# A convolution, attention and routing block on one core: the next pair's correlations put ahead of the logits, reciprocal deviations taken by a power on GpSimd, two norm groups summed back to back, fewer waits at the first K tile

## The reference

```python
def conv(x):                                  # x is the group-normalised input
    t1 = stack([pad(x)[..., 2*k:2*k+w] for k in range(7)])     # seven shifted copies
    t2 = conv_1x3(x, w2)
    t3 = einsum('nakhw,nbhw->nakb', t1, x) / sqrt(h*w)         # the correlations
    t9 = p9w * p6w * t3
    t10 = einsum('nakb,nakhw->nbhw', t9, shifted(t2)) / sqrt(c*7)
    return depthwise_5x5_dilated(x, w8) - (t10 - depthwise_1x5(t2, w7))
x = x + conv(group_norm(x))                   # 32 groups of 2 channels
t = tokens(x)
t = t + attention(layer_norm(t))              # 16 heads of 64; features elu+1 times cos, sin of
                                              # the position; keys x values summed over all tokens
t = t + ffn(layer_norm(t))                    # 32 experts: logits over all tokens, a softmax over the
                                              # tokens, the best 8 tokens of each expert are weighted
# layer_norm: (v - mean) / sqrt(var + eps) over the 64 channels of a token
```

## Time and profile before

| | us |
|---|---|
| median of 3 runs | 4075.51 (4073.82 to 4081.14) |
| the profiled execution | 4079.0 |
| its span, first to last instruction | 4077.2 |
| TensorE busy | 3586.0 (88%) |
| VectorE busy | 2994.3 (73%) |
| ScalarE busy | 1687.9 (41%) |
| GpSimd busy | 1248.6 (31%) |
| mean granted TensorE clock | 0.94 of full speed |

### The profile page before, as it was taken

How to read it: one execution, slowest core, us unless ns; L and a number is a source line. 1 busy time by engine, 2 the same in 40 slices (tenths; PEclk the granted TensorE clock), 3 DMA queues, 4 the chain that set the end, 5 groups by cost and what they waited for, 6 DMA issues and landing times.

```text
span 4077.2 us, 52073 instructions
## 1 busy us (share of the span) xinstructions
PE 3586.0 (88%) x17556; PEld 1798.3 (44%) x17556; DVE 2994.3 (73%) x3523; ACT 1687.9 (41%) x1798; POOL 1248.6 (31%) x1327
## 2 busy tenths in 40 slices
PE   4798998989889998989889899899989898899976
PEld 2344444444544444444444445344444444544453
DVE  6878876788677876788767886778767887548823
ACT  0145533455254534445434553445435554343310
POOL 1015620176013740156201760127501572011100
PEclk8899998999999998999989999999989999899967
DMA  1000000000000001000000000000010000100045
GB/s 47 17 1 1 1 17 25 1 1 1 25 17 1 1 1 41 1 1 1 17 25 1 1 1 25 17 1 1 1 41 1 1 1 16 30 1 1 1 116 200
DMA packets 18676, 70.96 MB, mean 17 GB/s; under 512 B 8781, under 2 KB 13421, under 8 KB 13485
## 3 DMA queue, kind: packets, MB, share of 16 engines
q1 hardware_dynamic: 18365, 67.10, 5.3%
HBM read 37.26 MB, written 29.84 MB: 16 GB/s over the span
## 4 chain that ended last, share of the span: by engine, by line
issue 48%; PE 33%; DVE 8%; POOL 7%; ACT 2%; DMA 1%; SPq 1%; POOLq 0%; DVEq 0%; ACTq 0%
PE ps_D L1499 11%; POOL UA L549 4%; PE ps_E L1463 4%; PE ps_C L1488 3%; PE ps_A L1446 3%; PE ps_B L1446 3%; DVE RR L1106 2%; PE ps_E L1474 1%; DVE region L1076 1%; DVE arena L911 1%; PE ps_C L1417 1%; POOL RS L581 1%; PE ps_E L1512 1%; POOL RR L574 1%; DVE region L1085 1%
## 5 line engine op out<-in xcount | busy, mean ns | idle before, releaser
L562 POOL TENSOR_TENSOR arena<-arena,UHL 128x896 f32<-128x896 f32 x350 | 764.6, 2210 | 226.3 <-ACT UHL L695 211.6
L1499 PE MATMUL ps_D<-region,small 128*128 128x448 f32 x1792 | 785.2, 562 | 32.9 <-DVE OS L1112 32.8
L549 POOL TENSOR_TENSOR UA<-region,CS 128x128 f32<-128x128 f32 (+1 forms) x400 | 178.8, 449 | 1837.8 <-DVE region L986 795.3
L1085 DVE TENSOR_TENSOR region<-region,ps_C 128x896 f32<-128x896 f32 x448 | 485.9, 1085 | 247.9 <-PE ps_C L1488 247.9
L1499 PEld LDWEIGHTS ps_D<-region,small 128*128 128x128 f32 x1792 | 321.2, 194 | 346.7 <-issue 284.8
L734 ACT ACTIVATE EQ<-ps_B,NEG 128x896 f32<-128x896 f32 x224 | 225.6, 1007 | 480.4 <-PE ps_B L1446 480.3
L911 DVE SCALAR_TENSOR_TENSOR arena<-arena,W8C 128x896 f32<-128x896 f32 (+1 forms) x418 | 416.8, 1010 | 1.2
L1417 PE MATMUL ps_C<-region,UA 128*128 128x512 f32 (+1 forms) x800 | 382.7, 601 | 2.9 <-ACT region L627 2.9
L734 ACT ACTIVATE EQ<-ps_A,NEG 128x896 f32<-128x896 f32 x224 | 225.6, 1007 | 350.8 <-PE ps_A L1446 350.7
L695 ACT ACTIVATE UHL<-arena,W8C 128x896 f32<-128x896 f32 x350 | 361.2, 1032 | 0.0
L1052 DVE SCALAR_TENSOR_TENSOR region<-region,ps_B 128x1024 f32<-128x1024 f32 (+1 forms) x200 | 243.9, 1219 | 159.8 <-ACT region L713 156.4
(11 more groups left out here) (310 smaller groups left out, 5772.9 us busy)
## 6 DMA issues: line engine op xcount, KB each, us to landing
arena<-x SPq DMA_DIRECT2D x8, 1568.0 KB, 6.6
t_keep<-Y SPq DMA_DIRECT2D x7, 1568.0 KB, 6.8
w_keep<-region SPq DMA_DIRECT2D x7, 784.0 KB, 5.7
CST<-t_keep SPq DMA_DIRECT2D x2, 1568.0 KB, 10.0
small<-t_keep SPq DMA_DIRECT2D x2, 1568.0 KB, 12.8
...
```

Source lines behind the costliest of these rows:

```text
L562: pool.tensor_tensor(out=X[:, cut], in0=X[:, cut], in1=PRODUCT[m % 3], op=ALU.add).then_inc(pool_taps.sem, 1)
L1085: dve.tensor_tensor(out=q, in0=q, op=ALU.mult, in1=here.area(key)[:, :].rearrange("p (c n) -> p c n", c=2)[:, :, 0:PIX])\
L1499: ins = pe.matmul(here.area(key)[:, 0:PIX], MW[i][:, c, :], Q[s % 3][:, c, :], start=c == 0, stop=c == NCHUNK - 1)
```

## The change

Six things change:

- **Correlations ahead.** In the loop, TensorE runs `correlations` (37 transposes and 124 matmuls) after the last slot of the Q loop, ahead of the tokens' transposes and logits; before, they came after the logits. ScalarE's copies (now `columns`) move with them.
- **The boundary's order.** TensorE no longer has the routing weights and the pooled tokens ahead of the convolution, but after its third part. VectorE does the residual of part 0 between match-replace and shares, that of part 1 after shares, then the sums of norm groups 0 and 1 back to back, then the scalings, and the residuals of parts 2 and 3 last. Its lower f16 half of group 1 moves into K tile 0.
- **Power on GpSimd.** All square roots on ScalarE and the reciprocals behind them on VectorE go. GpSimd computes variance + eps (a `tensor_scalar` of 128x14) and raises it to the power -0.5 (a `tensor_tensor` of 128x14); for the group norm VectorE adds eps and GpSimd takes the power of 128x1. Each power waits for the instruction ahead of it by the new semaphore `variance`.
- **Tiles of the K loop.** The sums of groups 2 and 3 start one tile later, the scalings stand at tiles 8 and 12 instead of 9 and 10, the f16 halves at 9 and 13 instead of 11 and 12, their transposes at 12 and 18 instead of 13 and 15, the group norm's application at 18 instead of 16, so that 31 instead of 33 pieces of the depthwise sums stand in the K loop.
- **Slots of the Q loop.** The scaling of the second norm stands one slot later (j - 7 for j - 6).
- **The wait at the K loop.** The first projection waits for banks D and E instead of A, B and C.

The diff, cut to its core:

```diff
-SUM_TILES = [None, None, 0, 4]
-STD_TILE = 8
-SCALE_TILES = [None, None, 9, 10]
-SPLIT_TILES = [None, None, 11, 12]
-UTS_TILES = [None, 2, 13, 15]
+SUM_TILES = [None, None, 1, 5]
+STD_TILES = [None, None, 6, 10]
+SCALE_TILES = [None, None, 8, 12]
+SPLIT_TILES = [None, 0, 9, 13]
+UTS_TILES = [None, 2, 12, 18]
...
-STATS_TILE, MEAN_TILE, CENTRE_TILE, VAR_TILE, NORM_TILE = 3, 12, 13, 15, 16
+STATS_TILE, MEAN_TILE, CENTRE_TILE, VAR_TILE, SPREAD_TILE, NORM_TILE = 3, 13, 13, 15, 16, 18
...
+
+            return [(("ucol", g), misc()) for g in range(len(COLGROUPS))] + [("t3", "D")]
+
...
-            uses += [(("wt", g), misc()) for g in range(2)] if routing else []
-            uses += [("t3t", misc())] + ([("pool", "E")] if routing else [])
-            for g in range(NG):
-                uses += [(("conv", g), misc())]
-                uses += [(("yt", g - 1), misc())] if g in (1, 2) else []
-                uses += [(("uts", i, 0), misc()) for i in range(2)] if g == 2 else []
-            return uses
+            uses = [("t3t", "C"), (("conv", 0), "A"), (("conv", 1), "B"), (("yt", 0), "C"), (("conv", 2), "A"),
+                    (("yt", 1), "B")]
+            uses += [(("wt", 0), "C"), (("wt", 1), "B"), ("pool", "E")] if routing else []
+            return uses + [(("uts", 0, 0), "D"), (("uts", 1, 0), "E"), (("conv", 3), "C")]
...
+            def deviations(sums, std, pair, g, turn):
+
+                pool.wait_ge(*sums.at(pair, g + 1))
+                passed(pool)
+                pool.tensor_scalar(ST[:, g % 2, 2, :], ST[:, g % 2, 1, :], 1.0 / C, LN_EPS, ALU.mult, ALU.add)\
+                    .then_inc(variance.sem, 1)
+                pool.wait_ge(*turn)
+                pool.tensor_tensor(out=ST[:, g % 2, 3, :], in0=ST[:, g % 2, 2, :], op=ALU.pow,
+                                   in1=NEGH[:, 0:1].broadcast_to([P, 2 * GROUP])).then_inc(std.sem, 1)
+
+            def group_norm(here):
+
+                pool.wait_ge(*here.emptied("gvar"))
+                pool.tensor_tensor(out=MV[:, 7:8], in0=MV[:, 6:7], in1=NEGH[:, 0:1], op=ALU.pow)\
+                    .then_inc(gn_scale.sem, 1)
...
                     ).then_inc(ua_ready.sem, 1)
+                    if k in STD_TILES:
+                        deviations(ln1_sums, ln1_std, pair, STD_TILES.index(k), variance.at(pair, STD_TILES.index(k) - 1))
+                    if here.span == "loop" and k == SPREAD_TILE:
+                        group_norm(here)
...
-                for j in range(SLOTS + POOL_LAG):
+                for j in range(ALL_SLOTS):
                     if slot_of_step(j, RECIP_LAG + 1):
                         split((j - RECIP_LAG - 1) // 4)
                     if here.span == "loop" and POOL_LAG <= j < POOL_LAG + POOL_PIECES:
                         tap_sum(j - POOL_LAG)
-
+                    if j - 5 in LN2_SLOTS:
+                        deviations(ln2_sums, ln2_std, pair, LN2_SLOTS[j - 5], variance.at(pair, 3 + LN2_SLOTS[j - 5]))
+                deviations(ln2_sums, ln2_std, pair, NG - 1, variance.at(pair, 2 + NG))
+                for g in range(2) if here.span == "loop" else ():
+                    deviations(ln1_sums, ln1_std, pair + 1, g, variance.at(pair, 3 + NG + g))
+
+            group_norm(Here("setup"))
+            for g in range(2):
+                deviations(ln1_sums, ln1_std, 0, g, variance.first(g + 1))
...
-            def group_norm(here):
-
-                act.wait_ge(*here.filled("gvar"))
-                act.activation(MV[:, 6:7], here.area("gvar")[:, 0:1], ACT.Sqrt, bias=EPS[:, 0:1])\
-                    .then_inc(*here.empty("gvar"))
...
-            def deviations(sums, std, pair, g):
-                act.wait_ge(*sums.at(pair, g + 1))
-                act.activation(ST[:, g % 2, 2, :], ST[:, g % 2, 1, :], ACT.Sqrt, scale=1.0 / C,
-                               bias=EPS[:, 0:1])\
-                    .then_inc(std.sem, 1)
...
+            def back(here, pair, routing):
+
                 if routing:
                     shares(here)
+                for g in range(2):
+                    tokens(here, 1, g)
+                if routing:
                     routing_weights(here)
                 for g in range(2):
-                    tokens(here, 1, g)
-                    if g == 1:
+                    high_part(pair, g)
+                    if g == 0:
                         split_tokens(here, 0)
-                    deviations(ln1_sums, ln1_std, pair, g)
-                    high_part(pair, g)
...
-                    if k == STD_TILE:
-                        for g in (2, 3):
-                            deviations(ln1_sums, ln1_std, pair, g)
-                    if k in SPLIT_TILES:
+                    if k in SPLIT_TILES[2:]:
                         high_part(pair, SPLIT_TILES.index(k))
                     if k in UTS_TILES:
                         split_tokens(here, UTS_TILES.index(k))
-                    if k == VAR_TILE and here.span == "loop":
-                        group_norm(here)
...
-                    if j - 5 in LN2_SLOTS:
-                        deviations(ln2_sums, ln2_std, pair, LN2_SLOTS[j - 5])
                     if here.span == "loop" and j in FRONT_SLOTS:
                         front(here, [FRONT_SLOTS[j]])
-                deviations(ln2_sums, ln2_std, pair, NG - 1)
+                if here.span == "loop":
+                    columns(here)
...
+            def group_norm_spread(here):
+                dve.wait_ge(*here.filled("gvar"))
+                dve.tensor_scalar(MV[:, 6:7], here.area("gvar")[:, 0:1], GN_EPS, None, ALU.add)\
+                    .then_inc(*here.empty("gvar"))
+
+            def group_norm_apply(pair):
+                dve.wait_ge(*gn_scale.at(pair, 1))
                 dve.tensor_scalar(g_window(4, 0, H), X.rearrange("p (h w) -> p h w", w=W),
                                   MV[:, 2:3], MV[:, 7:8], ALU.subtract, ALU.mult).then_inc(g_ready.sem, 1)
...
                 dve.wait_ge(*std.at(pair, g + 1))
-                link(dve.reciprocal(st[:, 3], st[:, 2]))
                 return dve.tensor_tensor(out=u, in0=u, op=ALU.mult,
                                          in1=st[:, 3].unsqueeze(2).broadcast_to([P, 2 * m, C]))
...
             def back(here, pair, before):
+
+                if before is None:
+                    depthwise(here, pair, 51)
+                    taps(here)
+                    depthwise(here, pair, FIRST_PIECES)
+                else:
+                    depthwise(here, pair, PIECES)
+                    taps(here)
+                    dve.wait_ge(*t_stored.at(before, 1))
+                    routing(here)
+                conv_residual(here, pair, 0)
                 if before is not None:
-                    routing(here)
-                    depthwise(here, pair, 7)
                     shares(here)
+                conv_residual(here, pair, 1)
+                norm_sums(here, 1, ln1_sums, 0)
+                norm_sums(here, 1, ln1_sums, 1)
+                norm1_scale(pair, 0)
+                low_part(pair, 0)
+                norm1_scale(pair, 1)
                 if before is not None:
-                    depthwise(here, pair, PIECES)
-                else:
-                    depthwise(here, pair, 51)
-                taps(here)
-                if before is None:
-                    depthwise(here, pair, PIECES)
-                if before is not None:
-                    dve.wait_ge(*t_stored.at(before, 1))
                     pooled(here)
-                for g in range(NG):
-                    conv_residual(here, pair, g)
-                    if g in (1, 2):
-                        norm_sums(here, 1, ln1_sums, g - 1)
-                        norm1_scale(pair, g - 1)
-                        low_part(pair, g - 1)
+                conv_residual(here, pair, 2)
+                conv_residual(here, pair, 3)
...
+                    if conv and k == SPREAD_TILE:
+                        group_norm_spread(here)
                     if conv and k == NORM_TILE:
-                        group_norm_apply(here)
+                        group_norm_apply(pair + 1)
...
-                    if j - 6 in LN2_SLOTS:
-                        norm_scale(2, ln2_std, pair, LN2_SLOTS[j - 6]).then_inc(un2_ready.sem, 1)
+                    if j - 7 in LN2_SLOTS:
+                        norm_scale(2, ln2_std, pair, LN2_SLOTS[j - 7]).then_inc(un2_ready.sem, 1)
...
             def back(here, pair, routing):
-                correlations(here)
+
+                turned_correlations(here)
+                conv(here, 0)
+                conv(here, 1)
+                for g in (0, 1):
+                    pe.wait_ge(*here.emptied(("conv", g)))
+                    passed(pe)
+                    to_tokens(here, 1, g)
+                    if g == 0:
+                        conv(here, 2)
                 if routing:
                     routing_weights(here)
-                turned_correlations(here)
-                if routing:
```

(6 more changed lines are left out.)

40 lines of the change are left out of this document (16 added, 24 removed).

## The result

The changed kernel takes **3947.25 us** (median of 4 runs, 3942.45 to 3951.21), the kernel before 4074.66 beside it (4 runs, 4068.33 to 4081.14). The ratio is 0.9687, with a 95% interval of 0.9667 to 0.9706: 127 us less. The forecast was 3965 us. The profiled execution has a span of 3942.9 us for 4077.2, with a mean granted TensorE clock of 0.954 for 0.940. ScalarE's table loads of 1.28 us have gone from 95 to 2.

The account below looks back on a forecast made before the run. TensorE, busy 3586.0 of 4077.2 us, bounds the kernel, taking turns with VectorE at boundaries. 93.5 + 25 - 7 - 4 - 1 = 106.5 off 4079.0 gives 3972.5, 3969 as median, less 4 for the clock: 3965 us, range 3945 to 3990.

Parts of the forecast that it names:

- K loops: Seven K loops: four TensorE waits, 4.5 us together, go; 0.9 us per loop left for crowding on VectorE; -25 us.
- Boundary: Last fold to K loop: 70.8 us instead of 86.9 (three times) and 82.1 (four times); 93.5 us saved.
- Q loops: Two depthwise pieces per pair move in from the K loop, 1 us a pair; table loads' going counted nothing; +7 us.
- setup and tail: Setup: group 1's tokens transposed behind convolution part 2, +4 us; last pair: last norm group uncovered, +1 us.
- the 4 us for the clock: Products behind a K loop's stall run faster where TensorE no longer waits: 4 us less in all.
- Power on GpSimd: Norms: 0.5 us each for variance and power, covered by other work except +1 us once in the last pair.
- (c): Rival: power is a slow routine of x us, costing 6x - 26 per pair; 4119 us at x of 8; chance 0.05.
- The rule of the Trainium skill: Certain VectorE instructions and GpSimd instructions reading SBUF exclude each other; each power blocks VectorE for its length, nothing at 0.5 us.
- The 6 us: Setup's group norm: first call into freshly loaded GpSimd code costs some 6 us, once, if the power is such code.
- (a): Rival: VectorE becomes the bound earlier; 3 us per boundary, whole K gain and 1 per Q loop lost; 4018 us; chance 0.19.
- (b): Rival: larger gain; parts at full clock, no wait left in K, Q loop gains 2 us; 3927 us; chance 0.12.
- (d): Rival: moved correlations only push the logits back 18 us; K gain alone remains, less setup and Q; 4065 us; chance 0.04.

Follow-up runs that it names:

- experiment 3: Changed kernel with the correlations and ScalarE's column copies back behind the logits: 4022.59 us, ratio 0.9868 to the kernel before.
- experiment 4: Kernel before, with only the next pair's correlations and their column copies moved ahead of tokens and logits: 4174.33 us, ratio 1.0234.
- experiment 8: Changed kernel with the last convolution part ahead of the pooled products instead of behind the f16 transposes: 3926.83 us, ratio 0.9635.
- experiment 9: Experiment 8's kernel with the boundary's second f16 transposes in bank B and the first projection waiting for D alone: 3909.31 us.
- experiment 2: Changed kernel with f16 transposes, group statistics and their banks, and group norm's application at their old K tiles, powers kept: 3988.39 us.
- experiment 6: Changed kernel with square roots on ScalarE, reciprocals on VectorE, the second norm's last root behind the column copies: 3969.22 us.
- experiment 7: Changed kernel with each 128x14 power on GpSimd done twice, once into a spare tile: 3985.24 us, ratio 0.9778.

## Why the prediction was right

The median 3947.25 lies within the stated range of 3945 to 3990, but only 2 us above its lower end. That it came so near is partly luck: the K loops gave 37 us more than their term, and the boundaries 16 less.

**Boundary, forecast -93.5, measured -77.5.** The mechanism held step by step: ucol at 575.96 (forecast 578.8, from a fold 2.6 us later), VectorE's chain from 605.2 (609.7) to the end of the pooled copies at 638.5 (642.2), seven boundaries alike within 2.3 us, whatever the pooled products' clock. Taking the moved correlations away costs 83.6 at the boundaries (experiment 3), and experiment 4 shows that it takes the new order too. That is where the prediction read the rows wrongly: it says that behind the logits the correlations covered nothing of this chain, but they ran beside VectorE's routing, and moving them alone costs 116 us. The sum stood, since the convolution took their place in the same step. VectorE's chain ended 1.1 us earlier than forecast, but from there to the K loop 7.9 us passed, not 4.9, so that the first boundary took 72.7 us, not 70.8. Two terms of this end were too small. The loop's turn, 1.8 us, was not in the sum, since in the trace of before the longer wait for the residual stood there. And the last part took 5.0 to 5.4 us at the lower clock, not 4.36. Experiments 8 and 9 show that this remainder is a matter of place: 4 to 6 us per boundary more can be had.

**K loops, forecast -25, measured -62.** This is the mis-sized term. Between the two profiled spans lie 134.3 us, where the forecast had 110.5: K gave 37 us more than its term, the boundaries 16 less, the Q loops 10 more, setup and tail 3.4 less, and the 4 us for the clock are within K's 37. (The median is 18 us under the forecast and not 24, since the profiled execution of before lay 4.3 us above its median, and that of after 2.6 below.) I summed four waits and took 0.9 us off per loop for crowding on VectorE. Nothing came of the crowding: the second K loop of after has one wait of 0.48 us, and TensorE's idle time in the K loops fell by 34 us, where the term had 25. The larger part missing is the clock: the time at the lower level fell by 50.5 us, which at half the speed is 25 us, and 34 and 25 are nearly the 62. The places of the f16 transposes and of the group statistics are worth 52.8, the square roots' going 14.6 (experiments 2 and 6; they overlap, and sum to more than 62).

**Power on GpSimd, forecast 0.5 us, measured 2.58** (and 0.21 for the variance beside it). Five times off, with little harm: the cover that the prediction named was there. VectorE waited 4.1 us in all for the first norm's groups, 0.5 a boundary, and 24.8 us for the last group of the second norm, which lies beside t3. Rival (c), 6x - 26 a pair, predicts less than nothing at x of 2.58, which fits, and 5.0 us a pair at the doubled power; experiment 7 cost 5.4. That the sums meet is in part chance: at the boundary the doubled power cost 3.3 us, where (c) has 1.8, and in the K loop, where (c) has 1.1, nothing. The rule of the Trainium skill that the prediction weighed here is answered under the hardware, below. The 6 us that it weighed for the first power are not seen: that power, at 65.56, took 0.56 us like the others of its size. But GpSimd had been idle for 53.9 us ahead of it, which could hide them.

**Q loops +7, measured -3.2.** The forecast charged two more depthwise pieces and nothing for the square roots' going. The first was right: with the pieces back in the K loop (experiment 2) the Q loops are 6.9 us shorter. The second was not nothing: square roots back at the new slots cost 15.0 (experiment 6), where TensorE waits 15 us more for VectorE and 6 less for GpSimd. The two would give -8; the other 5 stay open.

**Rivals.** (a) is out: VectorE is the chain at the boundary, but gave nothing back in K. (b), 3927, said rightly that next to no wait would be left in K, and wrongly that the last part would run at the full clock; that took experiment 8. (d) is refuted by experiment 3, which loses the boundaries' whole gain without the move; with experiment 4, each half of the change alone loses at the boundary, and only together they gain. ((d)'s own terms give 4062, not 4065.) The measured 3947.25 lies between forecast and (b).
